# A graph-network kernel on one core: zeroing a matrix two pieces at a time, with the key stores and one load moved to other places in the queues

## The reference

```
gathered = edge_weight[:, None] * x[edge_col]
neigh = segment_sum(gathered, edge_row, 3125)
out = x @ w_self + neigh @ w_neigh + bias
x = layernorm(x + out)
```

## Time and profile before

| What | Time |
|---|---|
| median of 3 runs | 4121.82 us |
| the profiled execution, its own time | 4121.78 us |
| its span in the trace | 4119.9 us |
| last piece of the zeroing issued / first scatter starts | 99.6 us / 126.53 us |
| first comparison of the marks | 107.58 us |
| last scatter into `t_w` starts | 650.29 us |

### The profile page before, as it was taken

One profiled execution on the slowest core, in us unless ns is written; L12 is line 12 of the kernel. 1 busy time (PEld: TensorE's weight loads), 2 busy tenths in 40 slices (PEclk: granted clock), 3 DMA queues, 4 the chain that ended last, 5 costly groups with the idle time before them and its releaser, 6 DMA issues. The chain is left out here.

```text
span 4119.9 us, 65409 instructions
## 1 busy us (share of the span) xinstructions
PE 3064.7 (74%) x16682; PEld 1859.7 (45%) x16683; DVE 2148.8 (52%) x5407; ACT 1554.6 (38%) x3260; POOL 2052.9 (50%) x2082
## 2 busy tenths in 40 slices
PE   1233776989888686668769966768765599899998
PEld 1122333567666333348644434644333344544544
DVE  2654001148888886563689956688656700301204
ACT  0176000068888464441026644026433600402303
POOL 1577777777770777731777770727776000000000
PEclk5555888999999798778989987879877699999999
DMA  9666633356775233436731112933352232232320
GB/s 398 227 190 182 188 112 94 97 128 139 135 206 140 86 106 105 137 101 243 219 106 27 27 27 70 291 110 106 105 162 86 96 95 90 70 96 64 95 83 32
DMA packets 328542, 521.94 MB, mean 127 GB/s; under 512 B 141966, under 2 KB 203111, under 8 KB 324677
## 3 DMA queue, kind: packets, MB, share of 16 engines
q1 hardware_dynamic: 217577, 309.55, 25.9%
q0 software_dynamic: 78896, 124.49, 11.2%
q10 hardware_dynamic: 31885, 85.88, 5.6%
HBM read 407.66 MB, written 115.58 MB: 127 GB/s over the span
## 5 line engine op out<-in xcount | busy, mean ns | idle before, releaser
L1027 PE MATMUL ps<-shared_sb,onehot 128*128 128x264 f32 (+1 forms) x1600 | 581.6, 472 | 170.7 <-DVE accum L2070 165.8
L1086 PE MATMUL ps<-score_sb,shared_sb 128*128 128x512 f16 (+1 forms) x3150 | 640.8, 364 | 17.3 <-DVE shared_sb L2099 17.2
L1305 ACT ACTIVATE onehot<-iota,drel 128x128 f32<-128x128 f32 x1248 | 381.3, 388 | 544.7 <-PE ps L950 326.9
L2070 DVE TENSOR_TENSOR accum<-accum,ps 128x264 f32 (+1 forms) x1248 | 527.7, 423 | 12.5 <-issue 5.4
L628 POOL DMA_INDIRECT t_w<-early_sb x391 | 399.4, 1021 | 221.9 <-DMA t_w<-accum 96.5
L1027 PEld LDWEIGHTS ps<-shared_sb,onehot 128*128 128x128 f32 x1600 | 288.8, 215 | 462.9 <-issue 212.8
L655 POOL TENSOR_SCALAR onehot<-iota,carry_d 98x512 bf16<-98x512 f32 x28 | 43.6, 1564 | 911.0 <-PE ps L1103 811.2
L1086 PEld LDWEIGHTS ps<-score_sb,shared_sb 128*128 128x128 bf16 x3150 | 308.8, 99 | 338.3 <-issue 11.4
L645 POOL DMA_INDIRECT t_adj<-counts,early_sb x391 | 385.3, 985 | 121.0 <-issue 118.9
L668 POOL DMA_INDIRECT shared_sb<-table,idx_a x384 | 364.0, 948 | 119.2 <-issue 116.6
L668 POOL DMA_INDIRECT score_sb<-table,idx_a x192 | 200.6, 1045 | 315.2 <-issue 148.4
(11 more groups left out here) (403 smaller groups left out, 5546.2 us busy)
## 6 DMA issues: line engine op xcount, KB each, us to landing
score_sb<-t_adj SPq DMA_DIRECT2D x105, 640.0 KB, 3.9
accum<-t_hot SPq DMA_DIRECT2D x208, 256.0 KB
t_w<-accum ACTq DMA_DIRECT2D x13, 3200.0 KB, 34.4
t_hot<-shared_sb SPq DMA_DIRECT2D x104, 256.0 KB
resid_sb<-t_w SPq DMA_DIRECT2D x25, 1024.0 KB
shared_sb<-t_key SPq DMA_DIRECT2D x98, 256.0 KB
t_adj<-accum ACTq DMA_DIRECT2D x40, 560.0 KB, 3.2
shared_sb<-t_adj SPq DMA_DIRECT2D x35, 640.0 KB, 9.2
```

What stands on the lines that cost most here:

```text
L1027: pe.matmul(ps[:, RING[(HU * h + u) % len(RING)], 0:w], onehot[:, h % 2 * HU + u, :], around[g][place(g, i, h)][:, u, 0:w], start=True, st ...
L1086: mm = pe.matmul(ps[:, 2 * (i % 3) + f, 0:w], h_gin[:, t, m, f * P:(f + 1) * P], ring["gin"][:, at % HOLD, c, 0:w], start=(t == 0 and m == ...
L1305: last = act.activation(onehot[:, h % 2 * HU + u, :], iota[:, 0:P], ACT.Abs, bias=drel[:, bass.ds(step + u, 1)], scale=-1.0)
L2070: dve.tensor_tensor(to, to, bank.unsqueeze(1), ALU.add).then_inc(step_acc, 1)
```

## The change

ScalarE issues the same 13 zeroing DMAs, but has at most two under way: from the third on, it first waits until the piece two before it has landed. Pieces alternate between two semaphores (`attr_in`), and ScalarE itself raises `w_zero` by one for each landed piece. The loop runs two steps past the last issue, so it ends when the last piece has landed. The pieces are also issued in another order, the last region first.

On SP, the 3200 KB load of `x_pad` into `hrows` leaves the head of the queue; ScalarE now issues it, behind its other input loads. The stores of `t_drel`, `t_hi` and `t_lo1` move behind the loop that reads the keys, and that loop waits only for the two stores of `t_key`.

`FIRST` goes from 18 to 28, so DVE makes all four comparisons for ten more quads, and ScalarE's loop zeroes `t_adj` in 35 larger pieces in place of 40. The order of the scatters differs only in its last two groups: quads 80 to 87 and 88 to 97, before 80 to 88 and 89 to 97.

```
-FIRST = 18
+FIRST = 28
+PIECES = WT // 2
+W_GROUP = 8
@@ SP
-            put(hrows[:, :, 0:D], a["x_pad"]..., done("ld_xh"))
             sp.wait_ge(*count("adj_rows", 1))
             put(t_key[0:ET, :]..., adj_t, done("key_out"))
             put(t_key[ET:S, :], no_key, done("key_out"))
-            sp.wait_ge(*count("keys", 1))
-            put(t_drel..., drow_b, done("key_out"))
-            sp.wait_ge(*count("keys", 2))
-            put(t_hi..., hi_b, done("rows_out"))
-            put(t_lo1[0:S, :]..., lo_rows, done("rows_out"))
-            put(t_lo1[S:S + UN, :], lo_rows[0:UN, 0, :], done("rows_out"))
-            sp.wait_ge(*count("key_out", 48))
+            sp.wait_ge(*count("key_out", 32))
             with sp.Fori(0, QUADS // 2) as i:
...
+            sp.wait_ge(*count("keys", 2))
+            put(t_drel..., drow_b, done("key_out"))
+            put(t_hi..., hi_b, done("rows_out"))
+            put(t_lo1[0:S, :]..., lo_rows, done("rows_out"))
+            put(t_lo1[S:S + UN, :], lo_rows[0:UN, 0, :], done("rows_out"))
@@ POOL
-                pool.wait_ge(*count("w_zero", 16 * (WT // 2)))
+                pool.wait_ge(*count("w_zero", PIECES))
@@ ACT
-            for part in t_w.rearrange(...):
-                act.dma_start(part, no_sums).then_inc(done("w_zero"), 16)
+            for n in range(PIECES + 2):
+                if n >= 2:
+                    act.wait_ge(attr_in[n % 2], 16 * (n // 2))
+                    act.sem_inc(done("w_zero"), 1)
+                if n < PIECES:
+                    act.dma_start(parts_w[(n - 1) % PIECES], no_sums).then_inc(attr_in[n % 2], 16)
             def compare(i, h):
...
             act.sem_inc(done("key_used"), FIRST + 2)
             act.sem_inc(done("same_act"), FIRST)
...
             act.dma_start(cols[:, :, :], a["x_cols"]...).then_inc(done("ld_x"), 16)
+            act.dma_start(hrows[:, :, 0:D], a["x_pad"]...).then_inc(done("ld_xh"), 16)
```

More of the change, by code:

```diff
@@ L281, in build @@
         key_in = [sem(f"key_in{h}") for h in range(2)]
-        in_four, so_far = attr_in + key_in, [0, 0, 16 * (QUADS // 2), 16 * (QUADS // 2)]
+        in_four, so_far = attr_in + key_in, [16 * len(range(h, PIECES, 2)) for h in range(2)] + [16 * (QUADS // 2), 16 * (QUADS // 2)]
         adj_in = [sem(f"adj_in{r}") for r in range(HOLD)]
@@ L340, in build @@
         counts_at = [2 * 16 * n for n in scattered]
-        w_order = []
-        for quads in [range(8 * m, 8 * m + 8) for m in range(10)] + [range(80, 89), range(89, QUADS)]:
-            w_order += [L0H * q + b for b in range(L0H) for q in quads if L0H * q + b < EDGES_T]
+        w_groups = [range(W_GROUP * m, W_GROUP * m + W_GROUP) for m in range(QUADS // W_GROUP - 1)]
+        w_groups.append(range(W_GROUP * len(w_groups), QUADS))
+        w_order = [L0H * q + b for quads in w_groups for b in range(L0H) for q in quads if L0H * q + b < EDGES_T]
         quads_by = []
@@ L400, in _ @@
             put(attr_w[:, :], a["attr_w"], done("ld_attrw"))
-            put(hrows[:, :, 0:D], a["x_pad"].rearrange("(t p) d -> p t d", p=P), done("ld_xh"))
             sp.wait_ge(*count("adj_rows", 1))
@@ L404, in _ @@
             put(t_key[ET:S, :], no_key, done("key_out"))
-            sp.wait_ge(*count("keys", 1))
-            put(t_drel.rearrange("(b q) e -> q b e", b=SB), drow_b, done("key_out"))
-            sp.wait_ge(*count("keys", 2))
-            put(t_hi.rearrange("(b q) e -> q b e", b=SB), hi_b, done("rows_out"))
-            put(t_lo1[0:S, :].rearrange("(b q) e -> q b e", b=SB), lo_rows, done("rows_out"))
-            put(t_lo1[S:S + UN, :], lo_rows[0:UN, 0, :], done("rows_out"))
             def on_each(t, first, n):
                 return t[bass.ds(first, n), :].rearrange("s e -> (s e)").unsqueeze(0).to_broadcast([P, n * P])
-            sp.wait_ge(*count("key_out", 48))
+            sp.wait_ge(*count("key_out", 32))
             with sp.Fori(0, QUADS // 2) as i:
@@ L422, in _ @@
                     sp.dma_start(wide_key[:, h, :], on_each(t_key, i * 2 * L0H + h * L0H, L0H)).then_inc(key_in[h], 16)
+            sp.wait_ge(*count("keys", 2))
+            put(t_drel.rearrange("(b q) e -> q b e", b=SB), drow_b, done("key_out"))
+            put(t_hi.rearrange("(b q) e -> q b e", b=SB), hi_b, done("rows_out"))
+            put(t_lo1[0:S, :].rearrange("(b q) e -> q b e", b=SB), lo_rows, done("rows_out"))
+            put(t_lo1[S:S + UN, :], lo_rows[0:UN, 0, :], done("rows_out"))
             put(weights_l1[:, :, 0:D], a["L1_gnn_W"].rearrange("(c p) n -> p c n", p=P), done("ld_w1"))
@@ L1220, in _ @@
             no_sums = flat_a[:, 5376:5376 + W_ZERO].unsqueeze(1).to_broadcast([P, 2 * NP // W_ZERO, W_ZERO])
-            for part in t_w.rearrange("(k p n w) o -> k p n (w o)", k=WT // 2, p=P, w=W_ZERO):
-                act.dma_start(part, no_sums).then_inc(done("w_zero"), 16)
+            parts_w = t_w.rearrange("(k p n w) o -> k p n (w o)", k=PIECES, p=P, w=W_ZERO)
+            for n in range(PIECES + 2):
[4 more added lines that the diff above has]
+                    act.dma_start(parts_w[(n - 1) % PIECES], no_sums).then_inc(attr_in[n % 2], 16)
             def compare(i, h):
@@ L1242, in _ @@
             act.dma_start(cols[:, :, :], a["x_cols"].rearrange("(c p) n -> p c n", p=P)).then_inc(done("ld_x"), 16)
+            act.dma_start(hrows[:, :, 0:D], a["x_pad"].rearrange("(t p) d -> p t d", p=P)).then_inc(done("ld_xh"), 16)
             with act.Fori(FIRST // 2, QUADS // 2) as i:
```

## The result

| | before | after |
|---|---|---|
| median | 4119.76 us (20 executions) | 4128.48 us (20 executions) |
| lowest and highest | 4112.95, 4123.08 us | 4121.56, 4132.03 us |
| ratio after / before | | 1.0022 [1.0016, 1.0028] |
| last data of the zeroing | 125.8 us | 113.9 us |
| first comparison of the marks | 107.58 us | 117.92 us |

The ratio makes it 9.1 us slower, between 6.6 and 11.5. The forecast was 5.7 us. That its time, 4127.5, lies only 1.0 us from the measured 4128.48 is partly luck: it was added to 4121.82, and the median of 20 executions before came out 2.1 us lower. The profiled execution of the changed kernel happened to be its fastest, 4121.56 us, so the two traces are equally long; what they say is in their stages, not in their spans. "Last data of the zeroing" is the end of its last DMA packet.

A forecast was written before the change was run, and what follows sets the result against it. The end of POOL's scatters, started by quad 7's sum, was taken to bound the kernel. Quad 7's +5.7 us, all other terms 0, on 4121.82 gave 4127.5 us; range for 8 in 10: 4119 to 4136.

The forecast's parts named there:

- The chain: First stage: zeroing and quad 7's sum set POOL's scatters; both later branches start at their end, whose shift shifts the kernel.
- The sense of the wait: ScalarE's new wait holds the raise of key_used until the last piece lands, so marks start later against the zeroing.
- Last landing: End of the zeroing: 112.1 by subtraction, 112.4 by addition, taken as 113 us.
- First comparison: DVE's first comparison of the marks: 113 + 0.3 for raises and step + 3.4 for a key read = 116.7, before 107.6.
- Quad 7: Its sum lets the eighth scatter go: 30.9 us after the first comparison, at 147.6, before 141.9, so +5.7 us.
- The other 383 scatters: POOL's scatters after the eighth: same count and same waits, put at 0, between -2 and +3 us.
- End of marks and start of the products: Marks end some 5 us later, PE's products can start about 12 us late; cost 0, hidden by PE's idling.
- Later stages (E): Later stages shift by less or more than the scatters, meeting other traffic: 3 to 4 us either way.
- Rival B: The zeroing queue runs dry at each handover, 2.4 us dead: 27 or 14 us, time 4142 to 4155; 9%.
- Rival C: Marks start at once; 28 key reads fall into the zeroing, which ends near 139: +6 us all the same; 2%.
- Rival D: Zeroing ends at 112 and scatters lose most of their 17.0 us of waiting: -8.3 us, time 4113.5; 5%.
- signs of being wrong: Among them: last scatter shifted otherwise than the eighth; a gap between the scatters' shift and the time's.

The follow-up runs named there:

- a_early: Changed kernel with the raises of key_used and same_act moved ahead of the zeroing loop: 4114.8 us, ratio to the kernel before 0.9966.
- after_2: The changed kernel unaltered, measured again beside the kernel before on an ordinary chip: ratio 1.0019 [1.0009, 1.0028].
- a_pieces_2: a_early, with each group of eight quads' scatters waiting only for the zeroed pieces it writes to: 4070.57 us, ratio to the kernel before 0.9861.
- a_ten_2: Changed kernel with key_used raised by ten ahead of the zeroing and by the rest behind it, ordinary chip: ratio to the kernel before 0.9971.

## Why the prediction held, and where its terms were off

- **The chain** (zeroing, quad 7, scatters, both branches behind them): right. The table of seven kernels shows that the time follows the last scatter. One reading in it was off: of the 13.8 us that POOL waited for the marks, 6.5 lie ahead of the sixth to the eighth scatter, not most of it; the other 24 waits are the 0.3 us that any scatter has ahead of it, so nothing hangs on it.
- **The sense of the wait**: right. The marks start later and not earlier; SP's 76.2 us stand on the raise of `key_used`. `a_early` shows that the wait behind the zeroing, not the landing of keys, was what held them.
- **Last landing, 113**: 113.9 in the trace (114.0 in the second), 0.9 late. **First comparison, 116.7**: 117.9. The read left 0.7 us after the last data (114.61 - 113.9) where 0.3 was charged; the raise itself is at 114.4, so most of it is from the data to the raise. The key read itself, 3.3 us, was as priced.
- **Quad 7, 147.6**: the eighth scatter left at 149.55, and by the same 0.44 us behind the copy (149.12, last fence below) the quad was summed at 149.1. From the first comparison it took 31.2 us and not 30.9. So the term "+5.7 us" measured **+7.2**; it was too small by 0.9 (landing), 0.3 (step to the read) and 0.3 (quads). The sign was forecast rightly. The size lay on the bound of 0.2%: the prediction gave 69% to a change within it and 25% to slower, and 0.22% was measured, with an interval that reaches to both sides of the bound.
- **The other 383 scatters, 0 (-2 to +3)**: -1.8 in the first pair of traces (5.4 - 7.2), +2.5 in the second (9.9 - 7.4). Zero on average, and the width right.
- **End of marks and start of the products**: forecast +5 and +12. In the first pair the last matmul of the marks moved by 13.5 us (418.2 to 431.7) and the first product by 18.2 (441.5 to 459.7), in the second pair by 6.3 (422.3 to 428.6) and 10.5 (445.2 to 455.7). So the terms were a few us small at most. The ten more quads on DVE are not the reason: quad 27 is summed 10.2 us later than before in the first pair and 9.1 in the second, as the first comparison was (10.3), and the pairs part only in the loop behind it. It cost nothing, as the gap of 36.85 us before the last products shows.
- **Later stages (E)**: in the first pair, the products and the row gathers of the second layer are still 5.4 to 5.6 us late, and from about 3080 us on the two traces run level again. That is why the spans are equal. In the second pair the shift grows instead, from 9.9 at the last scatter to 13.5 at the last matmul. The expectation of `after_2` named a stretch some 3 us longer as the sign of a loss in the later stages. It was 3.6 longer there (3461.5 against 3457.9), but 5.8 shorter in the first pair. Over the ten traces from ordinary chips it is 3448.9 to 3467.1 us, so two pairs do not show such a loss.
- **Rival B**: real, but only with one piece at a time, 1.9 us a handover and not 2.4. With two it is not there.
- **Rival C**: its condition is not met by the change. Its price was wrong in sign, from reads charged at 0.95 us, as read outside the zeroing, and 28 in number; had the change done what its words say, the forecast would have missed by 20 us.
- **Rival D**: zeroing at 112 did not happen, and the scatters' waits for landings went from 17.0 to 14.7 us, not to 4.

Two of the prediction's own signs of being wrong are half there: in the first pair the last scatter moved by 5.4 us and the eighth by 7.2, and the time by 9.1. What remains open: 5.4 to 9.9 us of shift at the last scatter is as close as two pairs of traces come to the 9.1 us of the medians; the 2 us between the eighth scatter's 7.2 and that are within the interval, and no run takes them apart.

## What to carry to other kernels

Before a wait is added or a load is taken out of the way, look at which instructions stand *behind* the wait on the same engine: here two raises of a counter, rows of 17 ns in the trace, made the difference between 9 us slower and 14 us faster. Limiting the queue to two large transfers cost no bandwidth here, but it moves the engine's next instruction from the last issue to the last landing, 26 us in this kernel. And where a consumer waits for "all of it is zero", ask first which part it touches: that wait was worth some 43 of the 57 us (`a_pieces_2` against `a_early`), more than all reordering around it.

## What the runs showed of the hardware

- **Two queues on the same DMA engines**: 256 KB of keys read beside the zeroing cost the zeroing 0.6 us each, which is their bytes at the rate of both together (414 GB/s); by packet time they take 0.70 us there, and about 0.95 without the zeroing. The shares of both queues come to 101%.
- **A scatter beside DVE work on SBUF**: a scatter issue of 0.96 us takes 1.67 to 3.12 us when one of DVE's 104x2048 operations runs. The issue does not slow in proportion; it ends a constant time after a DVE instruction does. In the changed kernel the one at 149.55 ends at 152.30:

```profile
146.06 1.22 DVE L1794 CAST score_sb<-shared_sb 104x2048 bf16<-104x2048 f32 x1
...
149.12 0.16 DVE L1812 CAST counts<-ps 128x4 f16<-128x4 f32 x1
149.19 2.27 DVE L1798 TENSOR_TENSOR shared_sb<-shared_sb,score_sb 104x2048 f32<-104x2048 f32 x1
```

  DVE ends at 151.46, so 0.84 us before; the scatter at 146.43 ends 0.82 us after DVE's cast (148.10 - 147.28), and the one at 126.98 in `a_ten_2` again 0.84 us after (129.74 - 128.90). The longest there, 3.12 us at 131.49, outlasts the cast by 2.4 us: behind the cast DVE goes straight on with four comparisons, and it ends 0.82 us after the last of them (134.61 - 133.79). The Trainium skill, SBUF — State Buffer, section "Who interferes with whom", describes this as an exclusive lock on a port pair that DVE and GpSimd share, and the constant distance agrees with a lock. The page expects it of casts, and of a TENSOR_TENSOR only against GpSimd's reads; here the TENSOR_TENSOR, with both inputs in SBUF, delays the scatter as fully as the cast does. That fits the page if the issue reads its offsets in `early_sb`; no run separates its reads from its writes.
- **A chip on which the marks ran 2.3 times slower** (6.8 against 2.96 us a quad in the mean) by stalls: 17 of 80 quads took 11 to 29 us each, in straight code as in the loop, while the DMA engines stood still; the relative effect of the change was the same (1.0018).
